# Seven of sixteen columns placed by products, two chunks weighted by one instruction, and roots between two passes on GpSimd

## What is computed

```python
x = _layernorm(x + _L0_gnn_ref(x, edge_index, edge_type_16, ...))   # messages, gated by edge
x = _layernorm(x + _L1_gnn_ref(x, ..., node_type_4, edge_type_8, src, dst))  # attention, 4 heads
x = _layernorm(x + _L2_gnn_ref(x, edge_index, W, a, Wo, bo))        # attention, 8 heads
x = _layernorm(x + _L3_gnn_ref(x, weight, src, dst, edge_type_8, edge_weight))

def _L2_gnn_ref(...):                       # the second attention, per head
    e = leaky_relu(s_src[src] + s_tgt[tgt])
    m = segment_max(e, tgt)
    ex = exp(e - m[tgt])
    denom = segment_sum(ex, tgt)
    msgs = h[src] * (ex / denom[tgt])[:, :, None]
    out = segment_sum(msgs, tgt) @ Wo + bo

def _layernorm(x, eps=1e-05):
    return (x - mean(x)) / sqrt(var(x) + eps)
```

## Time and profile before

| | us |
|---|---|
| median of 3 runs | 3634.98 |
| the runs | 3631.04 to 3635.08 |
| the profiled execution, its own time | 3634.52 |
| its span | 3632.7 |
| PE busy, share of the span | 2852.6, 79% |
| DVE | 2641.7, 73% |
| POOL | 2197.2, 60% |
| ACT | 1922.9, 53% |

### The profile page before, as it was taken

One profiled execution on the slowest core, in us unless ns is written; L12 is line 12 of the kernel. 1 busy time (PEld: TensorE's weight loads), 2 busy tenths in 40 slices (PEclk: granted clock), 3 DMA queues, 4 the chain that ended last, 5 costly groups with the idle time before them and its releaser, 6 DMA issues. The chain is left out here.

```text
span 3632.7 us, 59741 instructions
## 1 busy us (share of the span) xinstructions
PE 2852.6 (79%) x14869; PEld 1755.7 (48%) x14869; DVE 2641.7 (73%) x7559; ACT 1922.9 (53%) x6218; POOL 2197.2 (60%) x2264
## 2 busy tenths in 40 slices
PE   2578619999989699577777768599999998888885
PEld 1444305555556455354555535466666654333332
DVE  9899828999987455688888854599999955444444
ACT  0277705555552154377777743378887844333333
POOL 0687767777767532566666523677776312777774
PEclk9988859999999699699999989799999998565665
DMA  4334337888870488877776734777777634333335
GB/s 133 115 86 124 109 96 242 265 261 265 265 202 25 116 333 341 283 219 208 213 204 203 187 106 175 213 220 220 220 221 218 157 125 185 103 103 103 103 104 102
DMA packets 259351, 651.50 MB, mean 179 GB/s; under 512 B 65353, under 2 KB 114324, under 8 KB 252244
## 3 DMA queue, kind: packets, MB, share of 16 engines
...
## 5 line engine op out<-in xcount | busy, mean ns | idle before, releaser
L1976 POOL DMA_INDIRECT a_rows<-table,met x568 | 549.7, 968 | 280.9 <-issue 120.0
L3537 PE MATMUL ps<-rows_in,hot_w 128*128 128x256 f32 x832 | 444.8, 644 | 104.5 <-ACT hot_w L3499 57.6
L1275 POOL DMA_INDIRECT rows_in<-table,met x416 | 411.5, 989 | 144.1 <-issue 107.1
L3487 POOL DMA_INDIRECT rows_in<-table,met x416 | 403.9, 971 | 140.6 <-issue 120.0
L3562 DVE TENSOR_TENSOR xs<-xs,ps 128x256 f32 x416 | 175.3, 421 | 303.9 <-PE ps L3537 302.1
L778 POOL DMA_INDIRECT records<-rec,rows x283 | 323.5, 1143 | 101.7 <-issue 86.0
L3537 PEld LDWEIGHTS ps<-rows_in,hot_w 128*128 128x128 f32 x832 | 196.0, 289 | 353.4 <-ACT hot_w L3499 176.9
L3499 ACT ACTIVATE hot_w<-hot,met 128x128 f32<-128x128 f32 x416 | 166.8, 402 | 374.8 <-PE ps L3537 345.6
L2452 PE MATMUL ps<-a_rows,a_hot 128*128 128x260 f32 x1136 | 314.3, 402 | 23.5 <-DVE acc L2458 16.1
L1976 POOL DMA_INDIRECT xs<-table,met x264 | 255.6, 968 | 122.9 <-issue 54.5
L2458 DVE TENSOR_TENSOR acc<-acc,ps 128x520 f32 x416 | 287.5, 691 | 20.5 <-issue 15.0
...
## 6 DMA issues: line engine op xcount, KB each, us to landing
...
a_rows<-table,met POOLq DMA_INDIRECT x568, 3.8
```

The source lines that it names most:

```text
L1275: e.indirect_dma_start(self.rows[:, n % self.RING, 0:2 * D], None, self.table, bass.IndirectOffsetOnAxis(ap=self.b.met[:, n, R_SRC:R_SRC + ...
L1976: e.indirect_dma_start(self.row(n, 0, self.width), None, self.table, bass.IndirectOffsetOnAxis(ap=b.met[:, n, self.word:self.word + 1], ax ...
L3487: e.indirect_dma_start(self.rows[:, n % self.RING, :], None, self.table, bass.IndirectOffsetOnAxis(ap=self.b.met[:, n, R_REL:R_REL + 1], a ...
L3537: e.matmul(b.ps[:, n % self.BANKS, 0:D], self.hot_w[:, n % GRP_H, :], self.rows[:, n % self.RING, :], start=True, stop=True).then_inc(self ...
```

## The change

Four things change. (1) PLACED goes from 5 to 7, so in blocks 3 to 23 seven columns go through PE and nine are scattered. (2) In Attend2, `weigh_vector` weights two chunks with one instruction at every even chunk. (3) In both attention passes, `other` and `diag` move from DVE to ACT; `diag` stands right behind `keep_r` and before the exponentials, `other` is made as minus `open_hot` plus one, for the one row that PE reads. (4) In Outputs1 the roots go to GpSimd, tile by tile, as an add and a power of -0.5, and LAG goes from 7 to 4.

```diff
-PLACED, LAST_PLACED, FROM = 5, 3, 3
+PLACED, LAST_PLACED, FROM = 7, 3, 3
...
-                e.tensor_scalar(self.other[:, :], b.iota[0:H, :], d0, None, ALU.not_equal)
...
-                    e.wait_ge(self.kept_r, self.w0 + w)
+                    e.wait_ge(self.kept_r, 2 * (self.w0 + w))
...
-        def scale_in(w):
-
-            e.wait_ge(self.kept_r, self.w0 + w + 1)
-            e.tensor_scalar(self.diag[:, :], b.ident[0:H, 0:H], self.keep_r[:, :], None, ALU.mult).then_inc(self.chain, 1)
...
-                if n >= 0 and i == 0:
-                    scale_in(w - 1)
...
+                if w < NW and i == self.CHAIN["ends_in"][0] + 2:
+                    e.wait_ge(self.chain, self.chained(w, "open"))
+                    e.activation(self.other[0:1, :], self.open_hot[0:1, :], ACT.Identity, scale=-1.0, bias=self.b.ones[0:1, 0:1])
                 if w < NW and i == WIN - 2:
                     e.wait_ge(self.chain, self.chained(w, "fall"))
                     e.activation(self.keep_r[:, :], self.fall[:, :], ACT.Exp, scale=-1.0).then_inc(self.kept_r, 1)
+                    e.wait_ge(self.kept_r, 2 * (self.w0 + w) + 1)
+                    e.mul(self.diag[:, :], self.b.ident[0:H, 0:H], self.keep_r[:, :]).then_inc(self.kept_r, 1)
                     e.wait_ge(self.chain, self.chained(w, "below"))
...
-            e.wait_ge(self.chain, self.chained(w, "diag"))
+            e.wait_ge(self.kept_r, 2 * (self.w0 + w + 1))
...
-        row = self.group(n, 0)
+        if n % 2:
+            return
         if n % WIN == 0:
             e.wait_ge(self.exped, self.w0 + n // WIN + 1)
-        value = row[:, MH:GW2].rearrange("p (h f) -> p h f", h=MH)
-        e.tensor_tensor(value, value, row[:, 0:MH].unsqueeze(2).to_broadcast([P, MH, HID]), ALU.mult).then_inc(self.weighed_v, 1)
+        both = self.rows(self.slot(n), 2)[:, :, 0:GW2]
+        value = both[:, :, MH:GW2].rearrange("p s (h f) -> p s h f", h=MH)
+        e.tensor_tensor(value, value, both[:, :, 0:MH].unsqueeze(3).to_broadcast([P, 2, MH, HID]), ALU.mult).then_inc(self.weighed_v, 1)
...
-    TILES = 4
-    LAG = TILES + 3
+    LAG = 4
...
+        def root(t):
+
+            stat = self.stat[:, t, :]
+            e.wait_ge(*self.measured.at(t + 1))
+            e.tensor_tensor(stat[:, 8:9], stat[:, 7:8], self.b.eps[:, :], ALU.add).then_inc(self.rooted.sem, 1)
+            e.wait_ge(*self.rooted.at(2 * t + 1))
+            e.tensor_tensor(stat[:, 9:10], stat[:, 8:9], self.half[:, :], ALU.pow).then_inc(self.rooted.sem, 1)
...
         for t in range(self.RING):
             gather(t)
+        ahead = self.LAG
+        for t in range(ahead):
+            root(t)
         for t in range(NS):
             if t + self.RING < NS:
                 gather(t + self.RING)
+            if t + ahead < NS:
+                root(t + ahead)
             put(t)
...
-            e.activation(self.stat[:, a:z, 8], self.stat[:, a:z, 7], ACT.Sqrt, bias=b.eps[:, :]).then_inc(self.rooted.sem, 1)
...
-            e.reciprocal(self.stat[:, a:z, 9], self.stat[:, a:z, 8]).then_inc(self.inverted.sem, 1)
...
-            if t % self.TILES == 0:
-                e.wait_ge(*self.inverted.at(t // self.TILES + 1))
+            e.wait_ge(*self.rooted.at(2 * (t + 1)))
```

24 lines of the change are left out of this document (8 added, 16 removed).

## The result

The changed kernel takes 3570.89 us in the median of 4 runs (3565.56 to 3574.24), beside 3635.03 us for the kernel before (4 runs, 3631.04 to 3638.46): a ratio of 0.9826, with a 95% interval from 0.9813 to 0.9840. That is 64 us less. The forecast was 3571.5 us. Its span is 3570.0 us in the profiled execution, 62.7 us less than before.

What follows compares the result with a forecast made beforehand. Bounds: GpSimd in Ranking, nearly full PE and DVE in Attend2, the maximum's chain in Attend1. Ranking -46, Attend2 -12, Attend1 -1, Outputs1 -4 sum to -63: 3634.5 - 63 = 3571.5 us, range 3550 to 3600.

Steps and rivals of the forecast that it cites:

- The ground: stages add up: Whole kernel: stages stand one after the other, so each edited stage counts in full; -46 - 12 - 1 - 4 = -63 us.
- Ranking, the count and the pace: Ranking: 42 fewer scatters at 1.447 us, limited by DVE's places, 0.8 us more per block; L741 moves 515.85 to 467.
- Ranking, ACT: Ranking: 12 more L584 add 3.5 us a block, waiting covers all but 0.7; PE done at about 465.5.
- Ranking, the reload: End of Ranking: reload L1192, no longer hidden under DVE's wait, lasts to 478 and costs +2.5 us, ends 0 and 13.
- The rival that gave the reload precedence over L741: End of Ranking: L741 waits for the reload, Ranking gives -35 us, total 3582.5; chance 0.13.
- The second rival, the stretched scatters: Ranking: DVE's longer work keeps stretching scatters, GpSimd stays the bound to the end; -34 us, total 3583.5; chance 0.05.
- Second pass: Attend2: paired weighting and moves to ACT free DVE 0.9 us a window, 24 us; half taken, -12 us, -2 to -24.
- The halving: Attend2: half of DVE's 24 us taken, because PE is 92% busy and something else is late next; -12 us.
- First pass: Attend1: only `other` and `diag` move to ACT; -1 us, between -6 and +8.
- the sixth rival: Attend1: `diag` ahead of the exponentials is paid in full, +8 us and not -1, total 3580.5; chance 0.05.
- Outputs1: Outputs1: 4 us won at the start, 1 by inversions, 1 to 2 given back at the tail; -4 us, -7 to +6.
- the rival by which it would be the bound: Outputs1: GpSimd's root doesn't fit the step, stage longer by up to 0.6 us in 16 steps; no chance given.

## Why the prediction was right, step by step

**The ground: stages add up.** It held to 0.1 us in the traces before and after. The kernels with one edit, made to test it, could neither bear it out nor refute it. A chain of waits that covers only the last stage doesn't make earlier gains worthless, where every stage waits for the one before.

**Ranking, the count and the pace.** 1.447 us per scatter was 1.446 in the result. That DVE's places would bound the end was right, and the added 0.8 us per block too: block 23 at 444.3 against 445.3.

**Ranking, ACT.** Here the working was too kind. It had ACT covered except for 0.7 us and in step with DVE. ACT was busy for 157 of 160 us and its wait for the transfer was gone altogether. The number survived because 0.7 and 0.8 us were nearly the same; the experiment with eight columns shows that there was no room left. ACT's 60 scalings ended at 465.57, as the working had it (465.5), but it had PE done with them, since "PE has room". PE ended at 469.23, 3.7 us later: its last 18 products stood behind three small ones and ran in part at the half clock. So L741 came at 469.3 and not at 467, and waited for PE and not for the read-back, which was there 1.2 us earlier.

**Ranking, the reload.** The cover was named and its loss costed, but the term was too small: 5.7 us for 2.5. It was expected to last to 478 and to cost the read-back and the store some 1 us each. It lasted to 484.4. The read-back lost 0.5 us (4.0 for 3.5); the store and the row transfers behind it were hurt, 4.4 us up to L1294 and 1.3 more up to L1346, since the store's packets only start as the reload's run out. The rival that gave the reload precedence over L741 (3582.5) did not happen. The run with the early reload put the two together on purpose: L741 came 5 us late, not 13. The Trainium skill's section "Queues, rings and completion order" in "DMA: Bandwidth & Descriptors", by which engines take turns between queues, fits a delay of 5 us rather than 15, and a read-back that lands ahead of the reload's end (474.4 and 475.2). It doesn't explain the store from ACT's queue, whose packets started only as the reload's ended. No run here sets the order between queues any further.

**The second rival, the stretched scatters.** It was put at 0.05, and the cost of the stretching at nothing more, because GpSimd catches up before the end. That held: the scatters' mean went from 1143 to 1155 ns. The working gave the 1.90 us to L685 and L320, and saw the danger in the 42 added L677. Beside L677 alone a scatter takes 1.0 us, beside L677 and L685 up to 1.25; what costs is L320, which the change doesn't touch, and to a lesser part L671, which it makes longer. The Trainium skill ("SBUF — State Buffer", "Who interferes with whom") says that tensor_scalar in its fast modes shuts GpSimd's descriptor writing out until it ends. The trace agrees for the 128x2048 tensor_scalar of L685 (a scatter ends 0.83 us behind it), and no hold is seen beside those of 128x128 (0.96 us). The same section says that a tensor_tensor with both inputs in SBUF contends with what GpSimd reads there, but infers that it leaves descriptor writing alone, as it takes only the read side. The inference is contradicted here: 2.3 to 3.0 us instead of 0.96 beside a 128x2048 bf16 tensor_tensor with both inputs in SBUF. The measurement decides.

**Second pass.** -14.1 for -12, and the two-chunk instruction at a pitch of 0.60 us, as taken from the nearest row. The halving was a choice between PE's 92% and a wait of 24 us, and it was close in the sum only: the pairs gave 82% of what they free, the moves 38%. The text had no reason for treating them alike. It took PE's wait for DVE (24 us) as what there was to win and expected half of it to go; only 5.3 of 25.3 us went while the stage got 14.1 shorter. So that its number came near is in part luck. The mechanism it named is there in part: DVE waits for PE for 15.6 us now, against 1.6, so the next gain on DVE alone would probably bring less.

**First pass.** -1.0 for -1. What the instruction ahead of the exponentials costs is given back by what DVE no longer does; by itself it was 1.1 to 4.5 us in the one set that tried it, within what equal kernels differ by there, and not the 8 us of the sixth rival.

**Outputs1.** -6.6 for -4: the term was mis-sized at the start. The first table product came 21.3 us behind the first gather instead of 26.6, 5.4 us and not 4, and the second followed after 3.97 us, where it had been 5.90 before; the working hadn't looked at that step. The steps with an inversion fell from 4.20 to 3.98 us (1.1 us in all, as said), and 1.8 us came back at the tail, as said. GpSimd fits its root into the step with half a microsecond to spare, and the rival by which it would be the bound falls.
